# Row maxima subtracted by four 32-row matmuls for two key tiles at once, ahead of the scores, in an exact-softmax attention kernel

## The reference

```python
q, k = _rope(q), _rope(k)
sim = jnp.einsum('bhid,bhjd->bhij', q, k) * SCALE
attn = jax.nn.softmax(sim, axis=-1)
out = jnp.einsum('bhij,bhjd->bhid', attn, v)
```

## Time and profile before

| what | value |
|---|---|
| median of 3 runs | 1981.33 us (1979.59 to 1981.44) |
| the profiled execution: its time | 1980.87 us |
| the profiled execution: its span in the trace | 1979.1 us |
| busy share of the span | PE 95%, DVE 75%, POOL 70%, ACT 42%, PE weight loads 58% |
| mean granted PE clock | 0.977 of full speed |

### The profile page before, as it was taken

How to read it: one execution, slowest core, us unless ns; L and a number is a source line. 1 busy time by engine, 2 the same in 40 slices (tenths; PEclk the granted TensorE clock), 3 DMA queues, 4 the chain that set the end, 5 groups by cost and what they waited for, 6 DMA issues and landing times.

```text
span 1979.1 us, 28994 instructions
## 1 busy us (share of the span) xinstructions
PE 1879.4 (95%) x10916; PEld 1156.2 (58%) x10916; DVE 1491.2 (75%) x2032; ACT 823.2 (42%) x1078; POOL 1392.3 (70%) x640
## 2 busy tenths in 40 slices
PE   5979999949999999999999999999999999999879
PEld 4768899825555555555555555555555555555579
DVE  6969999777777777777777777777777777775444
ACT  4642333203444444444444444444444444444422
POOL 3754544406787878788787878788787878789933
PEclk9999999959999999999999999999999999999989
DMA  7640301110121131111122111112211111112565
GB/s 257 250 187 27 136 33 51 44 32 22 44 58 46 50 86 44 49 44 60 44 60 86 50 44 48 45 44 60 87 58 46 49 44 48 45 34 54 191 234 203
DMA packets 141563, 152.88 MB, mean 77 GB/s; under 512 B 41840, under 2 KB 97776, under 8 KB 141168
## 3 DMA queue, kind: packets, MB, share of 16 engines
q1 hardware_dynamic: 141424, 151.03, 24.2%
HBM read 95.95 MB, written 55.05 MB: 76 GB/s over the span
## 4 chain that ended last, share of the span: by engine, by line
PE 62%; DVE 20%; issue 6%; POOL 3%; DMA 1%; ACT 0%; SPq 0%; POOLq 0%; DVEq 0%
PE banks L994 17%; PE banks L1014 12%; PE banks L939 10%; PE banks L971 9%; PE banks L997 6%; DVE half_max L1067 3%; PE banks L1023 3%; PE banks L1486 3%; POOL acc L1189 3%; DVE q_lo L1112 2%; DVE k_lo L1112 2%; DVE h_scales L110 2%; DVE f_y L131 1%; DVE f_amax L109 1%; DVE f_y L134 1%
## 5 line engine op out<-in xcount | busy, mean ns | idle before, releaser
L1189 POOL TENSOR_TENSOR acc<-acc,prob 128x1024 f32<-128x1024 f32 x384 | 919.3, 2394 | 153.7 <-ACT prob L1215 125.2
L1067 DVE TENSOR_REDUCE half_max<-banks 128x2 f32<-128x1024 f32 x512 | 628.1, 1227 | 305.4 <-PE banks L971 305.4
L1215 ACT ACTIVATE prob<-banks 128x1024 f32<-128x1024 f32 x512 | 512.5, 1026 | 624.8 <-PE banks L997 624.8
L1014 PE MATMUL banks<-prob,v 128*64 128x512 f32 x2048 | 495.7, 605 | 0.0
L1189 POOL TENSOR_TENSOR acc<-prob,prob 128x1024 f32<-128x1024 f32 x64 | 152.7, 2386 | 180.8 <-ACT prob L1215 180.8
L1014 PEld LDWEIGHTS banks<-prob,v 128*64 128x64 f32 x2048 | 124.3, 136 | 240.4 <-issue 191.9
L971 PE MATMUL banks<-k_hi,q_hi 64*128 64x512 f32 x1024 | 235.8, 456 | 21.8 <-DVE half_max L1067 20.8
L939 PE MATMUL banks<-xT,wqk 128*128 128x512 f32 x768 | 218.3, 420 | 2.0 <-DVE k_lo L1112 2.0
L971 PEld LDWEIGHTS banks<-k_hi,q_hi 64*128 64x128 f32 x1024 | 98.3, 187 | 199.8 <-issue 150.7
L994 PE MATMUL banks<-q_hi,k_hi 64*128 64x512 f32 x1024 | 204.7, 395 | 1.3 <-ACT prob L1215 1.3
L994 PE MATMUL banks<-q_hi,k_lo 64*128 64x512 f32 x1024 | 203.5, 392 | 0.0
(11 more groups left out here) (121 smaller groups left out, 2204.2 us busy)
## 6 DMA issues: line engine op xcount, KB each, us to landing
v_scratch<-v_out SPq DMA_DIRECT2D x32, 512.0 KB, 2.6
wqk<-wp_scratch SPq DMA_DIRECT2D x32, 512.0 KB, 3.5
v<-v_scratch SPq DMA_DIRECT2D x32, 512.0 KB, 4.7
inv_rows<-inv_scratch SPq DMA_DIRECT2D x128, 128.0 KB, 3.3
o_scratch<-o_norm SPq DMA_DIRECT2D x64, 256.0 KB, 2.0
o_in<-o_scratch SPq DMA_DIRECT2D x8, 2048.0 KB, 12.1
xn_scratch<-p_xT SPq DMA_DIRECT2D x32, 256.0 KB, 2.9
xT<-xn_scratch SPq DMA_DIRECT2D x8, 1024.0 KB, 6.3
```

Of the source, the lines that this page charges most:

```text
L1014: ins = nc.tensor.matmul(o_ps[head * DH:(head + 1) * DH, :], v[s % 2][:, kt, at:at + DH], prob[n % SLOTS][:, head, :], start=kt == 0, stop ...
L1067: nc.vector.tensor_reduce(half_max[:, half % 2, :, t % GRP, part], m_ps[:, :, :], axis=AX.X, op=ALU.max, negate=True).then_inc(half_maxed, 1)
L1189: nc.gpsimd.tensor_tensor(acc[b][:, :, :], first, prob[n % SLOTS][:, :, :], ALU.add).then_inc(added, 1)
L1215: nc.scalar.activation(prob[n % SLOTS][:, :, :], s_ps[n % 2][:, :, :], ACT.Exp).then_inc(exp_done, 1)
```

## The change

The fourth product leaves `scores`. A new function `maxima(n)` gives units n and n+1 their row maxima together: four matmuls, each on one quarter of PE's rows (32) and all 128 columns, each into one of the four banks of `s_ps`. It is called at the end of a round for the two units of the next round, and starts the accumulation (`start=True`), so that the three remaining products of a unit all add to it. For this the rows of maxima must stand four times in `max_rows` rather than twice: `combine` writes `max_cols` with a second small reduction, and the constant `own` repeats every 32 rows rather than every 64. `maxima(n)` waits for `exp_done` of all units before n; `scores` no longer waits for it. The wait for `rows_done` moves with it. The numbers of matmuls and weight loads are unchanged: four and four for each two units.

```diff
+QUAD, QROWS = 4, P // 4
...
+        def maxima(n):
+
+            s, u = divmod(n, UNITS)
+            half, kt = divmod(u, QT)
+            if kt == 0:
+                pe.wait_ge(rows_done, 2 * s + half + 1)
+            if n:
+
+                pe.wait_ge(exp_done, n)
+            else:
+                pe.wait_ge(kept["h_done"], TILES)
+                pe.wait_ge(kept["h_high"], TILES)
+            for k in range(QUAD):
+                rows = slice(k * QROWS, (k + 1) * QROWS)
+                nc.tensor.matmul(s_ps[k // 2][:, k % 2, :], ones_r[rows, :], max_rows[half][rows, :], start=True, stop=False)
+
         def scores(s, u):
...
-            if kt == 0:
-                pe.wait_ge(rows_done, 2 * s + half + 1)
-            if n >= 2:
-
-                pe.wait_ge(exp_done, n - 1)
-            elif n == 1:
-                pe.wait_ge(kept["h_high"], TILES)
...
-                    nc.tensor.matmul(s_ps[n % 2][:, head, :], left[rows, keys], right[rows, queries], start=k == 0, stop=False)
-            for head in range(2):
-                rows = slice(head * DH, (head + 1) * DH)
-                ins = nc.tensor.matmul(s_ps[n % 2][:, head, :], ones_r[rows, :], max_rows[half][rows, :], start=False, stop=True)
+                    ins = nc.tensor.matmul(s_ps[n % 2][:, head, :], left[rows, keys], right[rows, queries], start=False, stop=k == 2)
             ins.then_inc(scored, 1)
...
                 if r == 4 and scoring(s + 1):
                     turn_max(s + 1, 0)
+                n = s * UNITS + 2 * r + 2
+                if 0 <= n < STEPS * UNITS:
+                    maxima(n)
...
-            cols = max_cols[half][:, :].rearrange("p (h n) -> p h n", h=2)[:, :, 0:GRP]
-            nc.vector.tensor_reduce(cols, half_max[:, half, :, :, :], axis=AX.X, op=ALU.min).then_inc(max_done, 1)
+            cols = max_cols[half][:, :].rearrange("p (k n) -> p k n", k=QUAD)[:, :, 0:GRP]
+            nc.vector.tensor_reduce(cols[:, 0:2, :], half_max[:, half, :, :, :], axis=AX.X, op=ALU.min)
+            nc.vector.tensor_reduce(cols[:, 2:4, :], half_max[:, half, :, :, :], axis=AX.X, op=ALU.min).then_inc(max_done, 1)
...
-    own = (np.arange(P)[:, None] % DH == np.arange(GRP)[None, :]).astype(np.float32)
+    own = (np.arange(P)[:, None] % QROWS == np.arange(GRP)[None, :]).astype(np.float32)
```

## The result

The changed kernel takes 2026.65 us (median of four, 2025.84 to 2027.51) against 1980.46 us before: a ratio of 1.0234, 95% interval 1.0216 to 1.0251. It is 46 us slower. The forecast was 2022 us and the range 2002 to 2060.

The account below looks back on a forecast made before the run. PE's own sequence was taken to bound attention. Removing 0.465 us, adding a 0.435 us quad and a 0.20 us wait gave 0.165 us a round; 248 rounds made 41 us on 1980.87, so 2022 us, range 2002 to 2060.

Parts of the forecast that it names:

- The quad: Four 32-row matmuls on PE at the round's end cost 0.435 us, against 0.465 us removed with two pairs.
- Both rivals about it: Four quarters overlap incompletely (two by two 2081 us; chance 0.18), or no switch between row counts is paid (1972 us; 0.10).
- the row of the guess ahead of the projection: PE trace where rows go from 64 to 128 at 128 columns: 0.34 us, 0.10 of it draining; evidence for a paid switch.
- the 3.07x: Skill page's speedup for four 32-row matmuls, not 4x: quad stream 0.30 us, time about 18 us over the sum.
- The wait of the second guess: A round's second guess on PE waits for DVE's reduction of the first, giving back 0.20 us a round.
- 0.54 + 1.23 + 0.05: Delay to the reduction's start, its length and the lag behind it; second guess's weights load at 1.82 us at the earliest.
- The rival that this stall would not be there: The reduction can start sooner, so the second guess does not wait: -0.03 us a round, 1974 us; chance 0.04.
- The exponentials: The quad's wait for both exponentials of its round costs nothing, with 0.5 us of cover in even rounds.
- Each 0.1 us would cost 25 us: Price put on each 0.1 us of quad waiting for the exponentials, were its cover gone.
- Nothing more is lost there.: Behind the stalled second guess, values, second reduction, `low`, sums and transpose shift together, with no further loss.
- the forecast's sum: Per round -0.465 + 0.435 + 0.20, 0.165 us before rounding; over 248 rounds 41 us, on 1980.87 giving 2022 us.
- 0.14 us of slack: Before the change, the second guess's weights loaded at 1.96 us, while the first reduction allowed 1.82.

Follow-up runs that it names:

- e8: Changed kernel with the four quarter matmuls issued twice in a row, the second four overwriting the first: 2084.49 us, 57.7 us over the changed kernel.
- e2: Changed kernel with the `maxima` call moved from the round's end to behind the opening guess, ahead of the first `scores`: 2020.88 us, ratio 1.0213 to the kernel before.
- e1: Changed kernel's place for the maxima, at the round's end, but as two pairs on 64 rows, `combine` and `own` as before: 2035.19 us, ratio 1.0284 to the kernel before.
- e6: Changed kernel with the DVE maxima reductions over 256 of each bank's 512 columns: 1939.97 us, 87 us under the changed kernel.
- e3: Changed kernel with `spread_rows` of rounds 1 and 5 ahead of the first `maximum`: 2020.33 us, ratio 1.0212 to the kernel before.
- e7: Kernel before the change with the DVE maxima reductions over 256 of each bank's 512 columns: 1947.17 us, 32 us under the kernel before.

## Why the prediction was right, and what it missed

**The quad: right.** The sum had load 0.11 + stream 0.23 + drain 0.10 = 0.435 us. Measured are 0.43 from the quad's load to the guess's, and e8 parts it into 0.23 of stream and 0.20 of the rest. Both rivals about it fall: four quarters do overlap in full, and the switch between 32 and 64 rows is paid, as the row of the guess ahead of the projection had said of another pair of shapes. The Trainium skill's page TensorEngine Tiling (Array Packing), section Key Properties, says that a change of tiling mode drains TensorE, and the traces of e2 and e8 agree for 64 and 32 rows. By the 3.07x of the Trainium skill's page TensorE: Matmul & The Clock Gate, section Measured speedup vs the span model, the stream would have been 0.30 us, as an estimate. The runs have 0.23, a full 4x against four matmuls of 0.232, and the measurement decides.

**The wait of the second guess: right, and shown.** 0.20 us were forecast from 0.54 + 1.23 + 0.05. The load comes at 1.82 as said. e1 has the wait without the quarters, e2 the quarters without the wait, and e6 takes the wait away from the changed kernel itself by shortening the reduction. The rival that this stall would not be there falls.

**The exponentials: right.** Over the whole changed kernel they end 1.4 us of PE's idle time before the quad (L990), all of it at a late exponential of the last step, where ACT had waited for a DMA. The kernel before has the same wait there, 1.3 us ahead of its scores, so it is no price of the stricter wait. ("Each 0.1 us would cost 25 us" was a slip: only the 128 even rounds have so little cover, which makes 13.)

**The step that failed.** The prediction says of what stands behind the stalled guess: "Nothing more is lost there." It followed the values, sums and transpose, which shift together with the guess, and left out the projection of rounds 1 and 5. This begins by waiting for `max_rows`, which DVE writes right behind the first reduction. That write is tied to the first guess and not to the second, so it does not move when the second guess and what stands behind it come 0.27 us earlier: 1.68 + 0.68 + 0.05 = 2.41 us into the round, while the projection could start at 2.26. The term is 0.15 us in two rounds of eight, and measures 0.17 (6.31 against 6.14); it makes 62 x 0.16 = 10 us. e3 takes it away and its step has the length of the forecast's sum. So the sum should have been 41 + 10 = 51 us, and the steps have 31 x 1.61 = 50. The median shows 46 to 47.5. That the time came within 5 us of the forecast is therefore luck in part: 10 us were missed, and both profiles of the changed kernel start attention 4 us early. The difference stands already at the first guess (396.7 us against 400.3 before), in a stage whose program is the same. Some 2.0 us of it are there at 380 us. The other 1.6 us are matmuls of the stage ahead (L751), which take 4.48 us from 387.78 on in the kernel before and 2.86 from 385.75 on in the changed one; the granted clock from 385 to 393 us is 0.79 of full speed in the first, so part of the stretch ran at the lower level (1.2 GHz), and 1.00 in the second. What set off either is open. The profiles of the other kernels begin their first guess anywhere between 396.1 and 400.3 us.

**On the place of the loss.** Of 1.61 us a step, 8 x 0.20 are the wait for DVE, 0.3 the wait for `max_rows`, and the quad itself brings 0.3 back. This change saves PE a stream, pays with nearly as much for the switch, and uncovers a DVE loop that had 0.14 us of slack.

## What to carry to other kernels

Before work is taken from between an instruction and the one that waits for another engine's answer to it, subtract it from that distance: here the second guess streamed 2.19 us behind the first, with the answer at 1.82 and an open load of 0.11 behind it the earliest was 1.93, and of the 0.465 us taken out only 0.26 could count. List every wait that hangs on the near end of the distance and not on the far one; those do not move with the rest. And price a packed matmul with the changes of shape around it: two streams made into one save 0.23 us, one change of shape more takes nearly all of that (e6 against e7 leaves 0.036), and two take more (e2). From this one would expect packing to pay where many such matmuls stand together, or where a change of shape stands on both sides already; no run here measured such a gain.

## What the runs showed of the hardware

- Four matmuls on quarters of the rows, each with 128 columns, 512 moving columns and a bank of its own, stream in 0.23 us (e8: 57.7 us for 256 more of such groups), as do two on halves and one on the full array; their four weight loads take the time of a pair's two (0.19 us recorded, and in e8 0.11 before the next four go in).
- A change between 64 rows and 32 costs 0.20 us, about what the one from 64 rows to 128 costs (guess into projection: 0.10 us of drain and 0.11 us of open load), though the columns stay at 128 (e2: 0.43 us from load to load each way).
- A DVE reduction of 1024 columns in PSUM takes 1.23 us and one of 512 columns 0.69, about 1.04 ns for each column more (medians 1226 and 693 ns).
